# Moving the weights of routed slots to fixed addresses, and another order at the experts' end, in a one-core decoder layer

## The reference

```
x = layernorm(x + mamba(x))                    # 1024 tokens x 128, two scan directions
x = layernorm(x + cross_attention(ctx, x))     # 8 heads x 128, over 6404 context rows + 1024 latents
x = layernorm(x + moe(x))
moe: xn = layernorm(x)*gamma + beta; probs = softmax(xn @ router_w)          # E = 8 experts
     topv, topi = top_k(probs, 2); topv = topv / sum(topv)
     out = sum over e: comb[:, e] * (silu(clip(gate)) * up) @ down_w[e]      # gate, up = xn @ gate_up_w[e], F = 512
     out = out + the same with one shared expert of F = 128
```

## Time and profile before

| | us |
|---|---|
| median of 3 runs | 1713.95 (1713.87 to 1714.21) |
| the profiled execution | 1712.44 |
| its span | 1710.5 |
| TensorE, mean granted clock over the span | 0.992 of full |
| experts: first gate product to the last down product | 1616.4 to 1699.4 |
| from there to the end of the span | 11.1 |

### The profile page before, as it was taken

The page is one execution under the profiler, slowest core; times in us unless marked ns, Lnnn a source line. Parts: engine busy times, 40 slices in busy tenths (PEclk is TensorE's granted clock), DMA queues, the critical chain, the costliest instruction groups (busy, mean ns, idle before and its releaser), DMA issues.

```text
span 1710.5 us, 31900 instructions
## 1 busy us (share of the span) xinstructions
PE 1662.9 (97%) x9115; PEld 849.7 (50%) x9115; DVE 1323.9 (77%) x2322; ACT 1069.7 (63%) x1310; POOL 875.1 (51%) x724
## 2 busy tenths in 40 slices
PE   6888999999999999999999999999999999999996
PEld 5754444444444444445454544444454545445585
DVE  7988988877777777777777777777777777777667
ACT  5545666666666666666666666666666666667664
POOL 4767992054454545454545445454545454542365
PEclk9989999999999999999999999999999999999998
DMA  5032110000000000000000000000000000000201
GB/s 185 2 61 73 56 42 0 1 1 1 1 0 0 0 0 0 0 0 0 0 1 0 0 1 0 1 0 1 0 1 0 1 0 1 1 0 1 56 27 43
DMA packets 33570, 23.84 MB, mean 14 GB/s; under 512 B 19615, under 2 KB 31139, under 8 KB 33110
## 3 DMA queue, kind: packets, MB, share of 16 engines
q1 hardware_dynamic: 32374, 20.48, 4.4%
q0 software_dynamic: 1120, 2.31, 0.4%
HBM read 15.27 MB, written 4.23 MB: 11 GB/s over the span
## 4 chain that ended last, share of the span: by engine, by line
PE 92%; DVE 5%; issue 1%; ACT 1%; POOL 1%; DMA 0%; SPq 0%; POOLq 0%; DVEq 0%; ACTq 0%
PE PS L1966 91%; DVE mxs L1820 1%; PE PS L2295 0%; POOL p_arena L856 0%; DVE w_arena L1272 0%; DVE w_arena L1459 0%; POOL w_arena L694 0%; DVE mv L1303 0%; PE PS L1975 0%; DMA vecs<-in_L_attn_b_conv_w 0%; DVE z_arena L1864 0%; DVE w_arena L1387 0%; ACT p_arena L1081 0%; DVE p_arena L1556 0%; SPq L463 0%
## 5 line engine op out<-in xcount | busy, mean ns | idle before, releaser
L801 POOL TENSOR_TENSOR p_arena<-p_arena 128x512 f16<-128x512 f32 x364 | 596.4, 1638 | 671.4 <-ACT p_arena L1081 671.4
L1072 ACT ACTIVATE p_arena<-PS 128x1024 f16<-128x1024 f32 (+1 forms) x480 | 484.4, 1009 | 507.3 <-PE PS L1966 507.3
L1966 PE MATMUL PS<-a_arena,z_arena 128*128 128x512 f16 (+1 forms) x2832 | 746.6, 380 | 1.7 <-DVE a_arena L1835 1.4
L1524 DVE TENSOR_REDUCE mxs<-PS 128x512 f32 (+1 forms) x900 | 599.5, 671 | 184.6 <-PE PS L1966 180.2
L1966 PE MATMUL PS<-p_arena,z_arena 128*128 128x512 f16 x2800 | 740.6, 379 | 0.4 <-ACT p_arena L1090 0.4
L1081 ACT ACTIVATE p_arena<-PS 128x1024 f32<-128x1024 f32 (+1 forms) x480 | 482.0, 1004 | 0.0
L1556 DVE TENSOR_TENSOR p_arena<-p_arena 128x512 f16<-128x512 f32 (+1 forms) x480 | 393.4, 820 | 86.9 <-ACT p_arena L1081 80.8
L1966 PEld LDWEIGHTS PS<-a_arena,z_arena 128*128 (+1 forms) x2832 | 274.4, 98 | 326.2 <-issue 1.9
L1966 PEld LDWEIGHTS PS<-p_arena,z_arena 128*128 128x128 f16 (+1 forms) x2800 | 271.6, 98 | 313.3 <-ACT p_arena L1090 0.9
L1966 PE MATMUL PS<-z_arena,a_arena 128*128 (+3 forms) x1024 | 353.1, 360 | 3.1 <-DVE mxs L1524 1.3
L1966 PEld LDWEIGHTS PS<-z_arena,a_arena 128*128 128x128 f16 (+1 forms) x1024 | 97.7, 98 | 125.1 <-issue 4.6
(11 more groups left out here) (332 smaller groups left out, 1011.1 us busy)
## 6 DMA issues: line engine op xcount, KB each, us to landing
w_arena<-in_L_ffn_gate_up_w SPq DMA_DIRECT2D x8, 512.0 KB, 3.8
p_arena<-in_ctx SPq DMA_DIRECT2D x2, 1600.0 KB, 8.3
w_arena<-in_L_ffn_down_w SPq DMA_DIRECT2D x8, 256.0 KB, 4.2
a_arena<-in_L_xattn_Wkv SPq DMA_DIRECT2D x1, 1024.0 KB, 6.2
a_arena<-xg_dram SPq DMA_DIRECT2D x12, 65.0 KB, 2.0
xg_dram<-VO SPq DMA_DIRECT2D x1, 715.0 KB, 7.2
xg_dram<-VO SPq DMA_DIRECT2D x1, 650.0 KB, 8.4
w_arena<-in_x SPq DMA_DIRECT2D x1, 512.0 KB, 4.2
```

What stands on the lines that cost most here:

```text
L801: g.tensor_tensor(Plo[:, r % 3, QB:2 * QB], P32[:, r % 2, QB:2 * QB], Phi[:, r % 3, QB:2 * QB], ALU.subtract).then_inc(pl_ready, 1)
L1072: s.activation(Phi[:, r % 3, 0:w], ps, ACT.Exp, scale=1 / SSC).then_inc(hi_ready, 1)
L1524: v.tensor_reduce(mxs[:, i, bass.ds(kb, 1)], PS[:, 6 + par, 0:w], AX.X, ALU.max).then_inc(mx_read, 1)
L1966: return t.matmul(o, l, r, start=start, stop=stop)
```

## The change

- SyncE loads the packed words in place of TensorE and copies the weights of each dynamic slot from their place in `w_arena` to a buffer at a fixed address: gate and up into `guest` (3 buffers, over the staging buffer of the weights), down into `guest_dn` (4 buffers, over freed memory in `p_arena`). Each copy is two DMAs, one for the high and one for the low part: 256 KB each for gate and up, 128 KB each for down. TensorE waits for them (`guest_loaded` before gate, `guest_down_loaded` before down) and has no computed addresses left.
- The copies of gate and up of the first three guests are issued before SyncE waits for the sorted rows, the first three down copies after the first gate product of the stage. From then on the order is: gate and up of guest k, once unit of guest k - 3 has its up product, then down of guest k, once down of guest k - 4 is done. Before each it waits until the copy two before has landed.
- The low part of unit 29 moves from GpSimd to VectorE. `front_added` is split in two: the first addition at step 29, the second behind the low parts of units 29 and 30. The statistics of tiles 4 to 6 move ahead of the last small additions. The two parts of `yt` are read in reverse order.
- The two routing weights of the last tile come from a Tanh in place of an Exp, a sum, a reciprocal and a product; the Silu on one element behind it goes.
- The last scales: ScalarE loads Sqrt's table behind its last `high` and takes the root; VectorE adds one Newton step (`newton`), as at the kernel's start.
- `ld_ctx` is renamed `ld_part` and serves the down copies too; those hunks are left out here.

```diff
@@ -69,6 +69,7 @@
 YRING = 4
+GUESTS, GUEST_DOWNS = 3, 4
 POOL0 = 2
@@ -108,7 +109,7 @@
     kind, a, _ = ORDER[u]
-    return u == LAST_UNIT or (kind == "slots" and a % 3 == 2)
+    return u >= LAST_UNIT - 1 or (kind == "slots" and a % 3 == 2)
@@ -278,6 +279,7 @@
         yst = take([YRING, D])
+        guest_dn = take([GUEST_DOWNS, 2, 4 * D], F16)
@@ -299,6 +301,7 @@
         stage = take([2, 2 * F + 4 * D])
+        guest = stage.rearrange("p b n -> p (b n)").bitcast(F16).rearrange("p (b k n) -> p b k n", b=GUESTS, k=2)
@@ -589,6 +592,18 @@
+        def guest_loaded(eng, k):
+            eng.wait_ge(ld_st[k % 2], 32 * ((E + 2 - k % 2) // 2 + k // 2 + 1))
+        def guest_down_loaded(eng, k):
+            eng.wait_ge(ld_part[k % 2], 16 + 32 * (k // 2 + 1))
+        def unit_of_guest(k):
+            return at_unit("slots", SLOT_TILES.index(("dynamic", k)))
         def stage_parts(par, dst):
@@ -648,14 +663,49 @@
                     sp.dma_start(b[:, 2 * FS:2 * FS + D], a["shared_down_w"]).then_inc(ld_st[e % 2], 16)
+            sp.wait_ge(et_ready, 1)
+            packs = [sp.value_load(packu[0:1, i:i + 1], min_val=0, max_val=E ** E - 1) for i in range(2)]
+            sp.wait_ge(stage_used, NPART * E + 2)
+            expert = [(packs[k // E] >> (3 * (k % E))) & (E - 1) for k in range(NDYN)]
+            def guest_down_moved(k):
+                if k >= 2:
+                    guest_down_loaded(sp, k - 2)
+                if k >= GUEST_DOWNS:
+                    sp.wait_ge(dn_ps, used_at(unit_of_guest(k - GUEST_DOWNS)) + 1)
+                for part, w in enumerate((DNhi, DNlo)):
+                    sp.dma_start(guest_dn[:, k % GUEST_DOWNS, part],
+                                 w.rearrange("p e i d -> p (e i d)")[:, bass.ds(expert[k] * (4 * D), 4 * D)]).then_inc(ld_part[k % 2], 16)
+            def guest_moved(k):
+                if k >= 2:
+                    guest_loaded(sp, k - 2)
+                if k >= GUESTS:
+                    sp.wait_ge(f_up, unit_of_guest(k - GUESTS) + 1)
+                e = expert[k]
+                for part, w in enumerate((GUhi, GUlo)):
+                    sp.dma_start(guest[:, k % GUESTS, part],
+                                 w.rearrange("p e c -> p (e c)")[:, bass.ds(e * (2 * F), 2 * F)]).then_inc(ld_st[k % 2], 16)
+            for k in range(GUESTS):
+                guest_moved(k)
             sp.wait_ge(sent, 16 * 2 * NF)
                                  xg_dram.rearrange("(i p) n -> p i n", p=P)[:, home(i):home(i) + w, :]).then_inc(xg_ld[k], 16)
+            sp.wait_ge(f_gate, 1)
+            for k in range(GUESTS):
+                guest_down_moved(k)
+            for k in range(GUESTS, NDYN):
+                guest_moved(k)
+                guest_down_moved(k)
             for k in range(YRING):
                 sp.wait_ge(y_sent[k], 16 * len(range(k, SLOTS, YRING)))
-            for k, r in enumerate(Y_TILES):
+            for k, r in reversed([*enumerate(Y_TILES)]):
                 sp.dma_start(yt[:, r.start:r.stop],
@@ -1098,7 +1148,10 @@
                     at = TILES[half]
-                    s.activation(ex[:, at], ex[:, at], ACT.Exp).then_inc(rt_a, 1)
+                    if half == 0:
+                        s.activation(ex[:, at], ex[:, at], ACT.Exp).then_inc(rt_a, 1)
+                    else:
+                        s.activation(ex[:, at], ex[:, at], ACT.Tanh, scale=0.5).then_inc(rt_a, 1)
@@ -1195,8 +1248,9 @@
                     half_act(1, 1)
-                    s.activation(rt[:, 5, 0:1], iota8[:, 0:1], ACT.Silu)
             high(LAST_UNIT)
+            s.activation(rt[:, 5, 0:1], iota8[:, 0:1], ACT.Sqrt)
+            root(5)
@@ -1642,6 +1696,11 @@
                     dve.wait_ge(rt_a, half + 1)
+                    if half == 1:
+                        share = 0.5 / (HS * WS)
+                        v.tensor_scalar(wts[:, 0, at], ex[:, at], -share, share, ALU.mult, ALU.add)
+                        settle(v.tensor_scalar(wts[:, 1, at], ex[:, at], share, share, ALU.mult, ALU.add))
+                        return
                     settle(v.tensor_scalar(wts[:, 0, at], ex[:, at], 1.0, HS * WS, ALU.add, ALU.mult))
@@ -1900,14 +1959,14 @@
-            def front_added():
+            def front_added(k):
                 rows = acc[:, r.start:r.stop]
-                dve.wait_ge(dn_acc, BY_DVE[number("shared", 1, NF - 1 - HT)])
-                dve.wait_ge(yt_ld[1], 16)
-                for k in range(2):
-                    settle(v.tensor_tensor(rows, rows, yt[:, r.start:r.stop, k], ALU.add))
+                if k == 0:
+                    dve.wait_ge(dn_acc, BY_DVE[number("shared", 1, NF - 1 - HT)])
+                    dve.wait_ge(yt_ld[1], 16)
+                settle(v.tensor_tensor(rows, rows, yt[:, r.start:r.stop, k], ALU.add))
@@ -1937,13 +1996,16 @@
                 side_work(u)
+                if u == LAST_UNIT - 1:
+                    front_added(0)
             hidden(LAST_UNIT)
-            front_added()
+            low_dve(LAST_UNIT - 1)
             low_dve(LAST_UNIT)
+            front_added(1)
+            out_stats(Y_TILES[1])
             for u in range(NUNITS, NUNITS + 6):
                     small_dve(kind, a, t)
-            out_stats(Y_TILES[1])
             dve.wait_ge(half_acc, 2)
@@ -1951,8 +2013,12 @@
             settle(out_stats([LAST_TILE]))
-            for piece in range(1, 6):
-                tile_norm(range(TC), 0, piece, twice=False)
+            for t in range(TC):
+                last = v.bn_aggr(mv[:, t, :], st6[:, t, :])
+            settle(last)
+            v.tensor_scalar(rs[:, 0, 0:TC], mv[:, 0:TC, 1], EPS, None, ALU.add).then_inc(sq_in, 1)
+            newton(5, first_of(TC))
+            v.tensor_tensor(rs[:, 3, 0:TC], rs[:, 3, 0:TC], rs[:, 1, 0:TC], ALU.mult).then_inc(xf_ready, 1)
             dve.wait_ge(xf_ready, 3)
@@ -2310,8 +2376,6 @@
                 return (units[0:1], units[1:2], units[2:3]) if len(units) == 3 else (units[0:1], [], units[1:2])
-            packs = []
@@ -2445,9 +2509,6 @@
                         pe.wait_ge(hot_read, 5)
-                    if st == TAIL + 3 and end:
-                        pe.wait_ge(et_ready, 1)
-                        packs.extend(t.value_load(packu[0:1, i:i + 1], min_val=0, max_val=E ** E - 1) for i in range(2))
                     if st == TAIL + 2 and not first:
@@ -2561,9 +2622,6 @@
-            GU_flat = [w.rearrange("p e c -> p (e c)") for w in (GUhi, GUlo)]
-            DN_flat = [w.rearrange("p e i d -> p (e i d)") for w in (DNhi, DNlo)]
-            expert = [(packs[k // E] >> (3 * (k % E))) & (E - 1) for k in range(NDYN)]
@@ -2595,14 +2653,6 @@
-            def expert_of(u):
-                kind, a, _ = ORDER[u]
-                if kind == "dense":
-                    return a
-                home_kind, k = SLOT_TILES[a]
-                return k if home_kind == "own" else expert[k]
             def rows_of(u):
@@ -2612,10 +2662,18 @@
-                e, (x_hi, x_lo) = expert_of(u), rows_of(u)
+                x_hi, x_lo = rows_of(u)
+                kind, a, _ = ORDER[u]
+                if kind == "slots" and SLOT_TILES[a][0] == "dynamic":
+                    k = SLOT_TILES[a][1]
+                    weights = [guest[:, k % GUESTS, part] for part in range(2)]
+                    if o == 0:
+                        guest_loaded(pe, k)
+                else:
+                    weights = [w[:, a if kind == "dense" else SLOT_TILES[a][1]] for w in (GUhi, GUlo)]
                 for blk in range(4):
                     at = F * o + blk * P
-                    hi, lo = (w[:, bass.ds(e * (2 * F) + at, P)] for w in GU_flat)
+                    hi, lo = (w[:, at:at + P] for w in weights)
                     c = bank[:, blk * P:(blk + 1) * P]
@@ -2636,9 +2694,17 @@
-                e, (hi, lo) = expert_of(u), hidden_parts(u)
+                hi, lo = hidden_parts(u)
+                kind, a, _ = ORDER[u]
+                if kind == "slots" and SLOT_TILES[a][0] == "dynamic":
+                    k = SLOT_TILES[a][1]
+                    guest_down_loaded(pe, k)
+                    weights = [guest_dn[:, k % GUEST_DOWNS, part] for part in range(2)]
+                else:
+                    e = a if kind == "dense" else SLOT_TILES[a][1]
+                    weights = [w[:, e].rearrange("p i d -> p (i d)") for w in (DNhi, DNlo)]
                 for i, at in enumerate(BLOCKS):
-                    dn_hi, dn_lo = (w[:, bass.ds(e * (4 * D) + i * D, D)] for w in DN_flat)
+                    dn_hi, dn_lo = (w[:, i * D:(i + 1) * D] for w in weights)
                     mm(o, hi[:, at], dn_hi, start=i == 0, stop=False)
```

(10 more changed lines are left out.)

## The result

The changed kernel takes 1702.27 us (median of 4 runs, 1701.74 to 1704.43), the kernel before, run beside it, 1713.91 (1712.88 to 1714.21): a ratio of 0.9939, 95% interval 0.9926 to 0.9951. That is 11.6 us less. The forecast was 1705.0, some 9 us less, with a range of 1701.5 to 1709.5: the result lies in the range, near its fast end.

A forecast was written before the change was run, and what follows sets the result against it. TensorE was taken to wait for its own sequencer's address work in the experts' stage. Gains of 6.2 + 1.5 + 0.4 + 0.9 = 9.0 us gave 1703.4, forecast as a 1705.0 us median, range 1701.5 to 1709.5.

The forecast's parts named there:

- The sequencer as what bounds the slots: Experts' stage, units 5 to 17: TensorE waits for its own sequencer's address instructions, an excess of 8.1 us.
- Term 1: Experts' stage: fixed addresses remove 193 register instructions; 12 steps take 27.7 us, 6.2 us won.
- the sum: Whole kernel: 6.2 + 1.5 + 0.4 + 0.9 = 9.0 us won.
- my ends of 3.0 and 8.1: Fixed addresses' gain: 3.0 us if the chain is late in most steps, 8.1 with TensorE at its pace.
- The copies at nothing: Experts' stage: SyncE's weight copies come in time, so TensorE's new waits for them cost 0.
- the margin of 0.8 us: Guest 9's gate and up: 5.8 of 6.6 us used, 0.8 to spare; the same for guests 7 and 11.
- The slow rival: SyncE's computed-address SBUF to SBUF issues set the stage's pace from 1.0 us each; at 1.3, about 1718 us; chance 0.05.
- Term 2: ScalarE before unit 21's Silu: Tanh in place of Exp needs no table load, 1.5 us won, ends 0 and 1.9.
- Term 3: Experts' end: new order of low parts and additions takes 3.0 against 3.6 us on VectorE; 0.4 us won.
- My end of -0.6: Order at the end: by full blocking both low parts end behind GpSimd's additions, making the term -0.6 us.
- Term 4: Last scales, epsilon to first row written: 1.6 in place of 2.50 us, 0.9 us won.
- One sign of being wrong: Start of the experts' stage: the forecast is wrong if it comes later than 1617 us.

The follow-up runs named there:

- experiment 8: Changed kernel with VectorE's low part ahead of its hidden in all steps: 1701.61 us, ratio 0.9935 to the kernel before.
- experiment 12: Changed kernel with VectorE's low part ahead of hidden, and low parts of slots 2 and 5 on GpSimd: 1701.68 us, ratio 0.9939 to the kernel before.
- experiment 10: Changed kernel with all low parts of the slots on GpSimd, VectorE keeping only units 29 and 30: 1705.47 us, ratio 0.9953 to the kernel before.
- experiment 1: Changed kernel with TensorE working out the dynamic units' addresses again and SyncE copying nothing: 1710.4 us, ratio 0.9982 to the kernel before.
- experiment 2: Changed kernel with TensorE working out addresses again while SyncE's copies run unread: 1709.71 us, ratio 0.9982 to the kernel before.
- experiment 3: Changed kernel without copies or waits for them, dynamic slot k reading expert k mod 8 at fixed addresses (output differs): 1703.91 us, ratio 0.9943 to the kernel before.
- experiment 7: Changed kernel with two buffers for gate and up of dynamic slots in place of three: 1703.44 us, ratio 0.9948 to the kernel before.
- experiment 4: Changed kernel with Exp, sum, reciprocal and product in place of Tanh, and the one-element Silu back: 1705.2 us, ratio 0.9952 to the kernel before.

## Why the prediction was right, step by step

**The sequencer as what bounds the slots: right, shown.** Putting the computed addresses back, with or without the copies, gives back 33.85 us to the 0.01; nothing else of the change does. The estimate of TensorE's own work, 25.7 us in 12 steps, was 0.3 too high. In the changed kernel the timeline has six breaks in it, 0.47, 0.17, 0.17, 0.36, 0.66 and 0.52 us from one start to the next, where 0.056 is the pace (0.22 at the last, which follows a matmul of 512 columns): 1.9 us lost, and 27.26 - 1.9 = 25.4.

**Term 1, 6.2: right in kind, 0.4 too small in these steps.** I forecast 27.7 us and 2 us of waiting; it was 27.26 and 1.9, so most of the 0.4 is TensorE's own work. That a low part of VectorE comes in the step in which it is wanted was right: three of the six breaks (0.17, 0.66, 0.52; 1.0 us lost) end with one, and experiments 8 and 12 remove them. That GpSimd is close to TensorE's need was right as well: two breaks (0.17 and 0.36; 0.4 lost) end with its low parts, and in experiments 8 and 10 they cost more. The sixth (0.47; 0.4 lost) ends with ScalarE's copy of turned rows at line 1234, which I had not named.

**What the sum left out.** I stopped counting at unit 17. Behind its down group five groups still had computed addresses, and they cost 0.5 to 0.85 us more; ahead of the 12 steps it was 0.15. With them the fixed addresses are worth 7.2 to 7.6 us (6.59 + 0.15 + 0.5 or + 0.85; experiment 1 has 7.2 for the whole stage), inside my ends of 3.0 and 8.1, but above the 6.2 that I took.

**The copies at nothing: right, and the margin of 0.8 us too, by luck.** Experiments 2 and 3 show it from both sides. I had named guests 7, 9 and 11 as tight; 9 and 11 have 0.9 and 0.6 us to spare, 7 has 3.2. The two terms of the margin were both too large. I had 6.6 us from issue to use and 5.8 until landing, with the two down copies of guest 8 queued in front. For guest 9 it is 4.85 and 3.94 (first issue at 1647.80), and those down copies were issued before, from 1645.24 on. With one buffer less TensorE waits for guests 7 and 9 (experiment 7). The issue itself was 0.51 us against the 0.43 to 0.48 I took from a plain one. The slow rival needed 1.0 and falls with that row.

**Term 2, 1.5: right.** 1.24 and 1.59 us in two surroundings. Nothing loads a table between Silu's load at 1616.32 us and Sqrt's at 1686.81, so Tanh is in the set that Silu's table brought. The Trainium skill (ScalarE: Activation LUTs, "Table sets: the hidden batching unit") lists tanh beside exp and beside sigmoid and has no line for silu. Read strictly, that spoke for a load here, and the measurement decides: there is none.

**Term 3, 0.4: right, 0.55.** From VectorE's last hidden to the end of its additions it was 2.85 us, forecast 3.0, before 3.56. The Trainium skill (SBUF — State Buffer, "Who interferes with whom") says that a VectorE instruction with two SBUF inputs contends with a GpSimd one that reads SBUF. The trace agrees: the first low part took 1.69 us and ended 0.55 behind GpSimd's second addition. My end of -0.6 took for granted that both low parts lie beside the additions; GpSimd, rid of unit 29, was through at 1687.37, and the second took 0.68.

**Term 4, 0.9: right, 0.89.** Two hops between the engines and five small steps in place of 12.

**The sum.** 9.0 forecast, 10.78 by spans. The 1.78 are: 0.51 of the start (the granted clock, not the change), 0.39 in the 12 steps, 0.15 before them, 0.59 behind them (the groups left out, and Tanh's own difference), 0.15 and -0.01 at the end. The medians moved 11.6, which is 0.9 more than the spans and within what runs of one kernel scatter. One sign of being wrong was badly chosen: the stage starting later than 1617. Five of the twelve kernels below the result do so, by the granted clock alone.

## What to carry to other kernels

An engine that counts as busy for 98% of a stretch can still be waiting for its own sequencer: compare the starts of equal groups, with fixed and with computed addresses, before believing the busy share. If a table of addresses is known early, an idle queue that copies the data to a fixed place can be cheaper than computing on the engine that sets the pace, even at 10 MB of traffic (26 DMAs of 256 and 26 of 128 KB). When the bound of a stretch goes, count the same cause behind it too, and take each change's worth from the stretch that it touches: here every term but the first was under the 0.2% that whole runs tell, and the trace gave them to about 0.1 us, the second to 0.3. A copy that comes in time once need not have room: read its landing and its use before the ring is made smaller or the pace faster.

## What the runs showed of the hardware

- Eight register instructions of 46 ns, two for each block of three matmuls of 128 columns, hold a group of 12 at 1.01 us in place of 0.67. 192 of them cost 6.6 us, 34 ns each, while TensorE shows hardly any idle time.
- A VectorE instruction with two SBUF inputs that meets a GpSimd one seems to get through when that one instruction ends, not when GpSimd falls idle. Before, GpSimd's two additions ran 1696.9 to 1700.1 and the low part, begun at 1697.4, was done at 1699.0, some 0.6 us behind the end of the first of them. In the changed kernel the low part begun at 1686.23 was done at 1687.92, 0.55 behind the end of the addition that ran then (spans of GpSimd are rough).
- The granted clock fell soon after the idle time of 2.16 us that TensorE now has before its last 24 products. The idle time alone doesn't do it: in experiments 4, 7 and 10 it is as long, and the clock stays at 1.00 through these 24. The fall cost nothing, since VectorE sets the end there: the stretch from the last 36 products to the epsilon is 7.86 to 7.88 us in all kernels with the new order, whether these 24 took 2.46 us (changed kernel), 2.11 (experiment 12), 1.81 (experiment 8) or 1.50 (experiment 10). The clock is the last but two of the columns, 0.50 (the level of 1.2 GHz) at the end:

```profile
1686.00:1688.00 2.00, 0.00 (x0) 0.00 (x0) 1.91 (x3) 1.98 (x3) 1.29 (x2) 1.00 0.00 0
1688.00:1690.00 2.00, 1.93 (x22) 1.97 (x23) 1.92 (x6) 0.30 (x2) 0.00 (x0) 0.60 0.00 0
1690.00:1692.00 2.00, 0.52 (x5) 0.25 (x3) 1.79 (x8) 0.00 (x0) 0.00 (x0) 0.50 0.00 0
```
